# A recurrent layer on one core: the decay product in two row waves, one sum moved into PSUM, and two queues reordered

## The reference

```python
xm = x[None] + xx[None] * (lo + time_maa)            # 4 mixed inputs, lo is low rank
xrg, xwa, xk, xv = xm[0], xm[1], xm[2], xm[3]
r = xrg @ Wr.T;  k = xk @ Wk.T;  v = xv @ Wv.T
g = jnp.tanh(xrg @ gate_w1.T) @ gate_w2
w2 = jnp.tanh(xwa @ decay_w1.T) @ decay_w2            # hidden size 64
w = -jax.nn.softplus(-(time_decay + w2)) - 0.5
kk = k + jnp.tanh(xk @ kkk_w1.T) @ kkk_w2             # then divided by its norm in each head
a = jax.nn.sigmoid(time_aaaaa + xwa @ aaa_w1.T @ aaa_w2)
ma = jax.nn.sigmoid(time_misc_a + xwa @ ma_w1.T @ ma_w2)
k = k * ma + k * a * (1.0 - ma)
mk = jax.nn.sigmoid(time_misc_k + xk @ mk_w1.T @ mk_w2)
k = k * jnp.exp(w * mk)
b = -kk * a
# per step and head: s = s*w + (s@kk) b^T + v k^T ; y = s @ r
```

## Time and profile before

| What | us |
|---|---|
| median of three runs | 1071.95 |
| lowest, highest | 1068.2, 1084.34 |
| the profiled execution, its own time | 1076.19 |
| its span, first to last instruction | 1074.1 |
| granted TensorE clock, mean of the span | 0.951 |

### The profile page before, as it was taken

How to read it: one execution, slowest core, us unless ns; L and a number is a source line. 1 busy time by engine, 2 the same in 40 slices (tenths; PEclk the granted TensorE clock), 3 DMA queues, 4 the chain that set the end, 5 groups by cost and what they waited for, 6 DMA issues and landing times.

```text
span 1074.1 us, 42156 instructions
## 1 busy us (share of the span) xinstructions
PE 980.1 (91%) x16652; PEld 801.8 (75%) x16653; DVE 768.0 (71%) x1793; ACT 519.9 (48%) x1081; POOL 613.1 (57%) x1135
## 2 busy tenths in 40 slices
PE   8898989999999989999999998679899999999995
PEld 5676777777777767777777776557899898989894
DVE  5766788889879778887688885266476666666663
ACT  4474576677677576676476783221122121212120
POOL 1088786788886787785867876810133333333321
PEclk9997999999999999998799998689999999999998
DMA  5113225225324225224143133746545445544430
GB/s 121 40 21 81 71 33 110 65 51 111 77 47 101 70 44 111 72 42 107 17 101 87 28 91 85 206 115 232 217 163 176 161 174 162 176 158 170 158 119 4
DMA packets 208894, 112.14 MB, mean 104 GB/s; under 512 B 172508, under 2 KB 192224, under 8 KB 208352
## 3 DMA queue, kind: packets, MB, share of 16 engines
q1 hardware_dynamic: 202352, 100.92, 35.0%
q0 software_dynamic: 3744, 8.40, 2.3%
q10 hardware_dynamic: 2640, 0.54, 0.3%
HBM read 85.57 MB, written 26.08 MB: 104 GB/s over the span
## 4 chain that ended last, share of the span: by engine, by line
PE 61%; DVE 14%; issue 8%; POOL 6%; DMA 5%; ACT 4%; DVEq 1%; SPq 1%; ACTq 0%; POOLq 0%
PE bank L576 16%; PE bank L970 12%; PE bank L983 9%; PE bank L662 6%; PE ry L983 4%; PE bank L718 3%; POOL arena L1914 3%; POOL arena L1911 3%; DVE bank L1389 2%; PE ry L692 2%; PE bank L594 1%; PE bank L622 1%; PE bank L950 1%; PE ry L698 1%; PE bank L740 1%
## 5 line engine op out<-in xcount | busy, mean ns | idle before, releaser
L576 PE MATMUL bank<-arena 128*128 128x256 f32 (+2 forms) x992 | 280.9, 422 | 22.4 <-DVE arena L1434 9.5
L1914 POOL TENSOR_TENSOR arena<-arena 128x30 f32<-128x30 f32 (+14 forms) x480 | 261.6, 545 | 37.6
L1911 POOL TENSOR_TENSOR arena<-arena 128x30 f32<-128x30 f32 (+14 forms) x480 | 250.5, 522 | 36.4
L576 PEld LDWEIGHTS bank<-arena 128*128 128x128 f32 x992 | 178.5, 203 | 67.9 <-issue 31.5
L970 PEld LDWEIGHTS bank<-arena 128*128 128x128 f32 x1248 | 146.8, 194 | 5.8 <-issue 3.0
L970 PE MATMUL bank<-arena 128*128 128x128 f32 x1248 | 147.5, 277 | 3.1 <-DVE arena L1820 2.5
L1498 DVE TENSOR_TENSOR arena<-bank,arena 128x512 f32<-128x512 f32 x128 | 79.5, 684 | 53.1 <-PE bank L662 53.1
L1302 ACT ACTIVATE arena<-arena 128x1 f32<-128x1 f32 x39 | 11.5, 294 | 178.6 <-DVE arena L1774 178.6
L983 PE MATMUL bank<-arena 128*128 x416 | 96.4, 385 | 0.1
L1945 POOL COPY arena<-arena 128x1 int32 (+1 forms) x39 | 7.1, 183 | 146.4 <-DVE arena L1838 146.4
L983 PEld LDWEIGHTS bank<-arena 128*128 128x128 f32 x416 | 76.9, 190 | 14.5 <-issue 4.9
(11 more groups left out here) (173 smaller groups left out, 1757.7 us busy)
## 6 DMA issues: line engine op xcount, KB each, us to landing
arena<-in_W SPq DMA_DIRECT2D x47, 1024.0 KB, 5.1
scr_n<-arena SPq DMA_DIRECT2D x64, 128.0 KB, 3.0
arena<-scr_n SPq DMA_DIRECT2D x16, 512.0 KB, 3.7
scr_u<-arena SPq DMA_DIRECT2D x16, 512.0 KB, 4.5
arena<-scr_u SPq DMA_DIRECT2D x62, 128.0 KB, 2.9
arena<-in_xTp SPq DMA_DIRECT2D x32, 132.0 KB, 4.0
arena<-in_x SPq DMA_DIRECT2D x64, 64.0 KB, 2.7
scr_x<-arena SPq DMA_DIRECT2D x64, 64.0 KB, 1.8
```

Source lines behind the costliest of these rows:

```text
L576: mm = pe.matmul(ring.tile(m, name)[0:rows, to], lhsT, rhs, start=(i == 0), stop=(i == len(terms) - 1))
L1911: inv_ok.inc(f"m{s}", TT(t, U[:, 0:s, s:s + 1].broadcast_to(shape), U[:, s:s + 1, s + 1:TB].broadcast_to(shape), ALU.mult))
L1914: inv_ok.inc(f"a{s}", TT(U[:, 0:s, s + 1:TB], U[:, 0:s, s + 1:TB], t, ALU.add))
```

## The change

- `decay_a_kk` no longer makes z with 128 rows. z's weights are split by rows 0 to 31 and 32 to 63. The first part is issued with a and kk, interleaved, the second with ma and mk in the new `decay_ma_mk`, behind the router. The second part adds onto the first in PSUM.
- The product kk of the hidden layer is added onto k's bank (k's product clears the bank only once), after ScalarE has copied k. VectorE's `sum_kk` is gone; ScalarE's new `keep_kk` copies the sum, and `square_kk` squares it from the bank.
- On TensorE, k comes before the gates, and the router stands between the two waves.
- `norms`, `centre_y` and `variance_y` issue two products of 256 columns instead of one of 512.
- Banks: the solve's first bank is 5 (a's) instead of 1, the logits' is 0 instead of 3, bk11 is in 1, and the router's ranks in 2.
- ScalarE's order after the second turned keys: a, logits, kk copy, kk square, z, sigmoid of z, ma, abs. `key_decay` and `growths` come before the keys bk11.
- VectorE: `decay_reads` (q) moves behind `bonus_terms` (rk).

```diff
-        proj = Stage(sem("proj"), [(1, "k z0 z1 sg a0 a1 ma0 ma1 abs sq sab mk0 mk1 ln lnss inv W ek iW0 iW1 v "
+        proj = Stage(sem("proj"), [(1, "k a0 a1 kk sq z0 z1 sg ma0 ma1 abs sab mk0 mk1 ln lnss inv W ek iW0 iW1 v "
                                         "vm0 vm1 tg")])
-        comb = Stage(sem("comb"), [(1, "kk scan t f k2 ls e2 kkn q ao bt k3 rk bm0 bm1 km0 km1 u wend")])
+        comb = Stage(sem("comb"), [(1, "scan t f k2 ls e2 kkn ao bt k3 rk q bm0 bm1 km0 km1 u wend")])
...
-                 "r": [(comb, "rk"), (comb, "q")], "v": [(proj, "v"), (proj, "vm1")], "kk": [(comb, "kk")], "ss": [(comb, "bm1")],
+                 "r": [(comb, "rk"), (comb, "q")], "v": [(proj, "v"), (proj, "vm1")], "kk": [(proj, "sq")], "ss": [(comb, "bm1")],
...
-        ring = Ring(banks, [(0, "bk00@5"), (1, "h@2"), (-2, "g@4"), (1, "k@3"), (0, "bk01@2"), (1, "z@1 a@5 kk@3 ma@4 mk@2"),
-                            (-3, "logit@3"), (-2, "wo@0"), (1, "ss@0"), (-1, "xa@1 xb@3"), (1, "r@4"),
-                            (0, "bk11@5"), (1, "v@2"), (0, "bk10@5 v0@1 v1@3"),
+        ring = Ring(banks, [(0, "bk00@5"), (1, "h@2"), (1, "k@3"), (-2, "g@4"), (0, "bk01@2"), (1, "a@5 kk@3"), (-3, "logit@0"),
+                            (1, "z@1 ma@4 mk@2"), (-2, "wo@0"), (1, "ss@0"), (-1, "xa@5 xb@3"), (1, "r@4"),
+                            (0, "bk11@1"), (1, "v@2"), (0, "bk10@5 v0@1 v1@3"),
...
             def decay_a_kk(m):
                 hid_act.wait(pe, m, "decay", "copy", "kkk")
-                from_hidden(m, [[("z", 2, slice(0, P), hid)]])
-                from_hidden(m, [[("a", 0, slice(64, 96), hid), ("kk", 0, slice(96, 128), kkh)]])
-
-            def ma_mk(m):
-                hid_act.wait(pe, m, "copy")
-                from_hidden(m, [[("ma", 1, slice(64, 96), hid), ("mk", 1, slice(96, 128), hid)]])
+                for name in ("z", "a", "kk"):
+                    ring.wait_empty(pe, m, name)
+                for h, to in both:
+                    mm_z = pe.matmul(ring.tile(m, "z")[:, to], w_out[0:32, 2, hs(h)], hid[0:32, :], start=(h == 0), stop=False,
+                                     skip_group_check=True)
+                    mm_a = pe.matmul(ring.tile(m, "a")[:, to], w_out[64:96, 0, hs(h)], hid[64:96, :], start=True, stop=True)
+                    mm_kk = pe.matmul(ring.tile(m, "kk")[:, to], w_out[96:128, 0, hs(h)], kkh[96:128, :], start=False, stop=True,
+                                      skip_group_check=True)
+                mm_z.then_inc(half_decay, 1)
+                ring.fill(m, "a", mm_a)
+                ring.fill(m, "kk", mm_kk)
+
+            def decay_ma_mk(m):
+                pe.wait_ge(half_decay, m + 1)
+                for name in ("ma", "mk"):
+                    ring.wait_empty(pe, m, name)
+                for h, to in both:
+                    mm_z = pe.matmul(ring.tile(m, "z")[:, to], w_out[32:64, 2, hs(h)], hid[32:64, :], start=False, stop=True,
+                                     skip_group_check=True)
+                    mm_ma = pe.matmul(ring.tile(m, "ma")[:, to], w_out[64:96, 1, hs(h)], hid[64:96, :], start=True, stop=True)
+                    mm_mk = pe.matmul(ring.tile(m, "mk")[:, to], w_out[96:128, 1, hs(h)], hid[96:128, :], start=True, stop=True)
...
-                fill(m, "ss", [(all_cols, [(head_sum, flat(nrm))])])
+                fill(m, "ss", [(to, [(head_sum, nrm[:, h])]) for h, to in both])
...
-                comb.wait(act, m, "kk")
-                proj.inc(m, "sq", A(flat(nrm), flat(kk), ACT.Square))
+                proj.inc(m, "sq", A(flat(nrm), bank(m, "kk"), ACT.Square))
+
+            def keep_kk(m):
+                if m:
+                    comb.wait(act, m - 1, "kkn")
+                ring.wait_full(act, m, "kk")
+                proj.inc(m, "kk", A(flat(kk), bank(m, "kk"), ACT.Copy))
...
                 if has(n + 1):
+                    keep_a(n + 1)
+                if has(n - 3):
+                    keep_logits(n - 3)
+                if has(n + 1):
+                    keep_kk(n + 1)
+                    square_kk(n + 1)
                     keep_z(n + 1)
                     sigma_of_z(n + 1)
-                    keep_a(n + 1)
                     keep_ma(n + 1)
                     abs_of_z(n + 1)
...
+                if has(n + 1):
+                    key_decay(n + 1)
+                    growths(n + 1)
                 if has(n) and n < last:
                     keep_keys(n, 1, 1)
-                if has(n + 1):
-                    key_decay(n + 1)
-                    growths(n + 1)
...
-                if has(n + 1):
-                    sum_kk(n + 1)
...
                     normed_kk(n + 1)
-                    decay_reads(n + 1)
                     decay_kk(n + 1)
                     removal(n + 1)
                     decay_keys(n + 1)
                     bonus_terms(n + 1)
+                    decay_reads(n + 1)
```

More of the change, by code:

```diff
@@ L570, in _, with fill @@
         def _(pe):
-            def fill(m, name, parts, cols=slice(0, HALF * COLS), rows=P):
+            def fill(m, name, parts, cols=slice(0, HALF * COLS), rows=P, started_once=False):
                 ring.wait_empty(pe, m, name)
-                for to, terms in parts:
+                for j, (to, terms) in enumerate(parts):
                     for i, (lhsT, rhs) in enumerate(terms):
-                        mm = pe.matmul(ring.tile(m, name)[0:rows, to], lhsT, rhs, start=(i == 0), stop=(i == len(terms) - 1))
+                        mm = pe.matmul(ring.tile(m, name)[0:rows, to], lhsT, rhs, start=(i == 0 and not (started_once and j)),
+                                       stop=(i == len(terms) - 1), skip_group_check=started_once)
                 ring.fill(m, name, mm)
@@ L612, in hidden @@
                 ring.fill(m, "h", mm)
[L614 to L623, removed]
-                                ring.fill(m, name, mm)
@@ L637, in square @@
                 xm_ok.wait(pe, m, f"x{x}")
-                fill(m, name, [(to, [(w_sq[:, w, k, hs(h)], xm[x][:, k]) for k in range(HALF)]) for h, to in both])
+                fill(m, name, [(to, [(w_sq[:, w, k, hs(h)], xm[x][:, k]) for k in range(HALF)]) for h, to in both],
+                     started_once=(name == "k"))
             def gate_1(m):
@@ L759, in centre_y @@
                 chain_act.wait(pe, m, "ye", "yo")
-                fill(m, "yc", [(all_cols, [(centre, flat(yc))])])
+                fill(m, "yc", [(to, [(centre, yc[:, h])]) for h, to in both])
             def variance_y(m):
                 post_act.wait(pe, m, "s")
-                fill(m, "var", [(all_cols, [(head_mean, flat(ysq))])])
+                fill(m, "var", [(to, [(head_mean, ysq[:, h])]) for h, to in both])
             def gates(m):
@@ L813, in body @@
                     keep_busy(1, ry_bank[0])
+                if has(n + 1):
+                    square(n + 1, "k", 1, 2)
                 if has(n - 2):
@@ L817, in body @@
                     keep_busy(2, idle_ps)
-                if has(n + 1):
-                    square(n + 1, "k", 1, 2)
                 if has(n) and n < last:
@@ L1258, in body @@
                     keep_x(n - 1)
-                if has(n) and n < last:
-                    keep_keys(n, 1, 1)
                 if has(n + 1):
@@ L1263, in body @@
                     growths(n + 1)
+                if has(n) and n < last:
+                    keep_keys(n, 1, 1)
                 if has(n) and n < last:
```

24 lines of the change are left out of this document (11 added, 13 removed).

## The result

The changed kernel is slower: 1105.66 us in the median of four runs (1101.55 to 1109.33) against 1074.9 of the kernel before on the same chip, 1.0302 times, with 1.0254 to 1.0350 as the 95% interval. Medians in this document are over all runs of a kernel, while ratios leave out runs more than 1.5% above their kernel's fastest, so the two can differ by up to 1%. The forecast was 1079, and the time lies above its range. Most of it is in the recurrent part: from the second body's scores to the last one's, fourteen bodies, one takes 42.36 us in the mean where it took 41.03. That makes 18.6 of the 25.4 us between the two profiled spans (1074.1 and 1099.5); the part behind the last scores, whose first tens of us are the last solve and read-out, takes 431.7 us for 426.4.

What follows compares the result with a forecast made beforehand. VectorE's chain to the last key product, then TensorE's scores, was taken to bound it, not TensorE's 91%. From 1076.19, +17.5 path, -12.6 and +3 clock gave 1084.1 profiled, 1079 for the median; range 1052 to 1098.

Steps and rivals of the forecast that it cites:

- The loop: Recurrent body: VectorE from mixing products to last key product L1445, then TensorE from scores to next mixing products, sets the pace.
- rival D: Decay waves on TensorE don't overlap: +0.86 us there within slack, under 2 us in all; no chance given.
- The step that was to decide: ScalarE's order: z's sigmoid comes late, VectorE's scan waits 2.1 us; with -0.60 and -0.67, +0.8 us a body.
- rival A: VectorE gets its sigmoid in time: -1.27 us for 16 bodies and -12.6 of clock, 1039 us; chance 0.12.
- my +0.95: VectorE's path to the last key product: +0.95 us for 13 blocks, some +1.7 for three, +17.5 us in all.
- TensorE's 0.86 us: Decay in two waves takes 0.86 us off TensorE per body, worth 0 on the path because of slack.
- the floor: Shortest recurrent body at full clock, some 39.3 us; bodies under it afterwards would show the prediction wrong.
- my sum: Whole change on the profiled execution: +17.5 us VectorE's path, -12.6 clock behind the router, +3 clock at the scores.
- -12.6 us of clock: Half-clock stretches behind the router, in four bodies, vanish as the router's wait goes: -12.6 us, bounds 0 and -12.6.
- The part on banks: TensorE waits 1.6 us before the v turns and 1.1 for q, at no cost; the solve no longer waits for the scan.
- Rival B: Clock falls in each body, TensorE stalling right before the scores: +13.5 us, 1091 to 1103 against the median; chance 0.22.
- q behind rk: VectorE's chain to the last key product gains one dependent neighbour pair: +0.17 us a body, range 0 to +0.35.

Runs made afterwards that it cites:

- sixth run: Kernel before with the two decay waves alone, ScalarE taking a before z, kk still summed on VectorE: 1085.82 us, 1.0129.
- fifth run: Changed kernel with the norms in bank 1 instead of 0, bk11 and the first v turns in bank 0: 1090.24 us, 1.0103.
- fourth run: Changed kernel with four idle products of 256 columns on TensorE between the solve's first half and the norms: 1096.53 us, 1.0251.
- tenth run: Kernel before with the three 512-column products in halves, alone: 1079.31 us, 1.0110.
- second run: Changed kernel with ScalarE's key_decay and growths back behind the keys bk11: 1119.97 us, 1.0467.
- thirteenth: Changed kernel with the norms in bank 1 and q back in front of ao, halved products kept: 1084.13 us, 1.0099.
- fourteenth: Changed kernel with the norms in bank 1 and the 512-column products whole again, q behind rk: 1080.45 us, 1.0072.

## Why the prediction was wrong

*Right.* The loop (VectorE to the last key product, then TensorE) held in the main, and three row groups overlap, so rival D is out. The step that was to decide did happen, which rules out rival A: 2.49 us before the scan for my 2.1, the sigmoid done 3.5 us behind a's start for my 3.6, the output add's wait gone. VectorE's way to the last key product grew by 0.86 us a body, for my +0.95. That TensorE's 0.86 us is worth nothing was not put to the test: the sixth run saved it, but with a late sigmoid.

*Near by luck.* The two bodies at full clock are 1.0 us above the floor in the mean, but one takes 41.5 us and the other 39.1, under the 39.3 that I named as a sign of being wrong. With the norms' bank changed the loss is 0.7 to 1.0%, 8 to 11 us, where my sum was +7.9. That sum holds -12.6 us of clock, and the fifth run's profile has more half clock than the kernel before (64.9 us for 54.6).

*The norms' bank, the step that failed first.* The part on banks priced the waits before the v turns and before the bonus product, and said "The solve no longer waits for the scan". It has no term for the norms, so they stood at nothing without a reason. The solve moved free of the scan, but the norms between its halves write bank 0, which the output add empties, and the output add stands behind the scan. I followed the late scan down VectorE's queue to L1412 and priced the output add by its own wait, and never asked who waits for the bank that it frees. That wait is 17.6 us in eleven bodies where the kernel before has 0.9 once, and half clock comes behind it. Moving the norms to another bank takes the ratio from 1.0302 to 1.0103 (fifth run). The waits that I did price came in that run (10.4 and 14.7 us), and hardly in the changed kernel (0 and 2.6).

*The clock.* I took -12.6 us for the half clock behind the router and added 3 at the scores. The front's half clock did go, from 20 to 1 us. But behind the solve it grew from 21 to 64 us, a stretch for which my sum had only a term taken away. The total rose by 34 us. Rival B had the direction, but its place, the scores, grew only from 14 to 24, and the time lies above its 1103.

*q behind rk, mis-sized when it stands alone.* I allowed +0.17 us a body, 3 us in all. Alone in the kernel before it measured 1.6%, some 17 us: besides the pairs of neighbours (0.81 and 0.80 us from start to start in the changed kernel, where others have 0.60) it takes away the 0.6 us that covered the key decay. The growths' move, which I read as a mere change of TensorE's waits, removes that wait; with it q measured 1.05%, though the intervals overlap, and inside the changed kernel nothing that can be told.

*ScalarE's late copies.* The last key product to the scores was 0.52 us and became 1.15. I had the scores start when L1445 ends. In eight bodies they wait for the value copies (L1175). ScalarE's logarithm of the norms stands ahead of these and waited 0.87 us for the norms in the body shown. With the norms in bank 1 the 1.15 us are down to 0.73.

*How much is clock.* Within the kernel before (33 runs beside the last experiments) a run with 0.01 less clock takes 6.7 us more. The changed kernel's four runs have 0.932 in the mean against 0.953 of those 33, so some 14 of its 31 us go with the clock. The rest would be the longer chain. That is a correlation, and its slope differs from kernel to kernel: a longer wait can lower the clock and adds its own time, and the fourth run, which gave the clock back with the wait still there, bought 5 to 9 us, where the fifth bought some 20 by the ratios. The exact split stays open, and so do the tenth run's 1.1% and the solve's longer waits for the inverse.

## What to carry to other kernels

When a wait is added on an in-order engine, follow every buffer that the operations behind it set free, not only the engine's own next waits: the costly waiter here was on another engine, on a bank that the diff left where it was. An order written out by hand is a set of matched pairs (q with the growths, the logits' bank with the place of their copy in ScalarE's queue), and one move undone may cost more than all together (1.0467 for 1.0302 in the second run), so measure the parts both ways, added to the old kernel and taken out of the new. Work taken off the busiest engine brought no gain in any run here, and idle work put into its waits bought about half a per cent at best, never by a margin well clear of noise.

## What the runs showed of the hardware

- Idle products raise the clock. Two of them ahead of the router took the kernel before from 0.949 to 0.964 in the mean of the runs and 0.5% off its time; four in the changed kernel took the profiled execution from 0.932 to 0.957. The Trainium skill's page TensorE: Matmul & The Clock Gate, section Part 1, has the gate follow how busy the array was just before. These runs agree, and so does the direction of the changed kernel's clock (0.951 to 0.932), though it fell behind the solve and not at the scores, where the second rival had it.
- Behind waits of 1.07 and 0.80 us around the solve's first half in the body shown, the norms and the second half ran at half clock, the latter in 1.93 us for 1.13.
- Within a kernel 0.01 less clock goes with 6.7 us more in 33 runs of the kernel before, with 13 us in ten of the fifth, and with 4 to 5 us in those of the thirteenth and fourteenth (ten and twelve). That is a correlation, and what clock alone is worth isn't shown.
- In the bodies shown, VectorE's operations of 512 columns start 0.78 to 0.81 us apart where one waits for the one before it (L1483 to L1467, L1472 to L1494 to L1478), and 0.60 where it doesn't. It is no fixed figure: L1422 to L1424, which also wait, start 0.70 us apart (524.58 and 525.28).
- Products of 32 rows in three row groups, into three banks, run at the same time: each first wave's record starts within 0.02 us of its two neighbours, and the twelve records of that wave start in four groups, 0.21 to 0.32 us apart.
